# Fetching 54 of a graph kernel's gathered tiles row by row from SyncE and ScalarE

## The reference

```python
h = jnp.maximum(_layernorm(x, axis=-1), 0.0)
# layer 1: mean of h[src] over each node's edges, beside h itself, times W
# layer 2: theta = h[dst] - h[src]; w = sigmoid(relu(theta @ W1 + b1) @ W2 + b2)
#          segment_sum(w * theta, dst) + indeg * (h @ W4 + b4)
# layer 3: mean of relu(h @ Wp.T + bp)[src], linear, elu, normalised by row
# layer 4: all_h = einsum('ni,rio->rno', h, weight)
#          segment_sum(all_h[etypes, src] * norm, dst) + h @ loop_weight
```

## Time and profile before

| What | Value |
|---|---|
| Median of 3 runs | 5245.48 us (5244.3 to 5245.74) |
| The profiled execution: its own time | 5255.77 us |
| Its span | 5253.4 us |
| Busy: PE, DVE, ACT, POOL | 73%, 56%, 30%, 70% of the span |
| Layer 2's gathers | from 976.9 us |
| Layer 4's gathers | from 3685.7 us to 5241.6 us |

### The profile page before, as it was taken

The page is one execution under the profiler, slowest core; times in us unless marked ns, Lnnn a source line. Parts: engine busy times, 40 slices in busy tenths (PEclk is TensorE's granted clock), DMA queues, the critical chain, the costliest instruction groups (busy, mean ns, idle before and its releaser), DMA issues.

```text
span 5253.4 us, 75208 instructions
## 1 busy us (share of the span) xinstructions
PE 3851.4 (73%) x22393; PEld 2977.7 (57%) x22393; DVE 2942.4 (56%) x9882; ACT 1575.8 (30%) x5791; POOL 3668.8 (70%) x3899
## 2 busy tenths in 40 slices
PE   3889999665666556566665488879899999999544
PEld 3345555655565555555555455445677777777443
DVE  7998876665555566666666744444544433333232
ACT  5555443433333333333333401132112222221000
POOL 5345553677777777777777477757777777777776
PEclk7799999877777777877778799989999999998655
DMA  4234443555555555555555556556111111111222
GB/s 124 69 123 141 145 145 125 166 156 158 157 157 157 157 156 158 159 159 158 159 161 161 153 191 201 200 178 244 52 50 51 51 51 50 51 51 52 53 73 53
DMA packets 303264, 663.89 MB, mean 126 GB/s; under 512 B 70592, under 2 KB 152924, under 8 KB 293388
## 3 DMA queue, kind: packets, MB, share of 16 engines
q0 software_dynamic: 155152, 369.61, 25.7%
q1 hardware_dynamic: 145692, 288.54, 16.3%
q10 hardware_dynamic: 2016, 0.92, 0.1%
HBM read 545.40 MB, written 113.38 MB: 125 GB/s over the span
## 4 chain that ended last, share of the span: by engine, by line
POOL 48%; PE 21%; issue 17%; DVE 9%; DMA 2%; ACT 2%; DVEq 1%; SPq 0%; ACTq 0%; POOLq 0%
POOL rows L1535 40%; POOL third L1535 8%; PE ps L2721 6%; PE ps L2618 3%; PE ps L2706 3%; PE ps L2630 2%; PE ps L2679 2%; DVE tmp L2019 2%; PE ps L2567 1%; PE ps L2686 1%; DVE oneh L1928 1%; DVE turned_words L2020 1%; DVE rows L2020 1%; DMA rows<-tab_hp,idx_src 1%; ACT h L1710 1%
## 5 line engine op out<-in xcount | busy, mean ns | idle before, releaser
L1535 POOL DMA_INDIRECT rows<-tab_rel,third x1203 | 1190.4, 990 | 366.7 <-issue 364.0
L1535 POOL DMA_INDIRECT rows<-tab_hp,idx_src x1120 | 1083.5, 967 | 345.2 <-issue 335.9
L2744 PE MATMUL ps<-third 128*128 128x128 f32 x3126 | 626.4, 363 | 729.4 <-DVE third L2049 728.7
L1535 POOL DMA_INDIRECT rows<-tab_h,idx_src x790 | 772.2, 977 | 541.2 <-PE ps L2686 276.2
L2744 PEld LDWEIGHTS ps<-third 128*128 128x128 f32 x3126 | 548.3, 264 | 790.5 <-DVE third L2049 789.5
L1758 ACT ACTIVATE turned_words<-turned_words 128x128 f32<-128x128 f32 x1563 | 463.2, 297 | 1251.0 <-DVE turned_words L2062 1251.0
L2721 PE MATMUL ps<-third,h 128*128 128x385 bf16 (+1 forms) x3626 | 742.7, 335 | 44.3 <-DMA h<-cnt_d 24.6
L2679 PE MATMUL ps<-oneh,rows 128*128 128x128 f32 x2406 | 403.2, 320 | 262.8 <-DMA rows<-tab_rel,third 160.1
L2679 PEld LDWEIGHTS ps<-oneh,rows 128*128 128x128 f32 x2406 | 352.5, 225 | 330.3 <-issue 183.2
L1535 POOL DMA_INDIRECT third<-tab_hp,idx_src x443 | 426.9, 964 | 135.0 <-issue 133.8
L2721 PEld LDWEIGHTS ps<-third,h 128*128 128x128 bf16 x3626 | 351.5, 100 | 293.8 <-issue 29.6
(11 more groups left out here) (305 smaller groups left out, 5685.6 us busy)
## 6 DMA issues: line engine op xcount, KB each, us to landing
third<-dst_flat SPq DMA_DIRECT2D x390, 256.0 KB, 3.5
cnt_d<-h SPq DMA_DIRECT2D x37, 1568.0 KB, 5.8
h<-cnt_d SPq DMA_DIRECT2D x37, 1568.0 KB
tab_rel<-third SPq DMA_DIRECT2D x49, 512.0 KB, 3.1
rows<-tab_rel,third POOLq DMA_INDIRECT x1203, 2.5
rows<-tab_hp,idx_src POOLq DMA_INDIRECT x1120
rows<-tab_h,idx_src POOLq DMA_INDIRECT x790
third<-tab_hp,idx_src POOLq DMA_INDIRECT x443
```

Of the source, the lines that this page charges most:

```text
L1535: pool.indirect_dma_start(out=to[:, t, 0:n], out_offset=None, in_=table[:, :], in_offset=bass.IndirectOffsetOnAxis(ap=idx[:, col:col + 1], ...
L2744: last = pe.matmul(ps_t[sl][:, t * P:(t + 1) * P], onehT[:, sl, t * P:(t + 1) * P], pwin[:, st["v"] % 2, :], start=True, stop=True)
```

## The change

In 37 groups the last tile is no longer gathered by POOL, but fetched by SP: 19 in layer 2 (groups 20, 40, ... 380) and 18 in layer 4 (groups 108, 124, ... 380). In 17 more groups of layer 4 (116, 132, ... 372) ACT fetches it. In the 17 turns up to two turns before such a group, each turn has a step `single_rows`: load eight indices from one partition into eight registers, then eight DMAs of one row each, with the row's address from its register, into a staging tile (two for each engine and layer). At the group's own turn a step `single_copy` waits for all 128 rows and for the slot, and copies the tile into its slot with one DMA. The users of the group, DVE's `hidden` in layer 2 and PE's scatter, wait for that copy (`s_moved`) too. The indices come by small DMAs of SP: 19 before layer 2's first window, and 35 in the step `late` ahead of the loads that were there, each of 128 single words, one from each partition's row of `parked[0]`. In layer 4 the row work lies in each of the 16 turns between one single tile and the next, in layer 2 in 16 of 20.

```diff
+SINGLES = {1: (("sp", 20, 20),), 3: (("sp", 18, 16), ("act", 26, 16))}
+ROW_LOAD = 8
...
+            def single_rows(g):
+                for who in singles:
+                    for j, at in enumerate(singles[who]):
+                        r0 = (g - (at - P // ROW_LOAD - 1)) * ROW_LOAD
+                        if 0 <= r0 < P:
+                            if r0 == 0:
+                                single_full[who, j] = s_single[layer, who][j % 2].up(16 * P)
+                            free = n_moved[singles[who][j - 2]] if j > 1 and r0 == 0 else None
+                            plan.append(("single_rows", dict(layer=layer, who=who, j=j, r0=r0, free=free)))
...
             for turn in range(turns):
                 tails[:] = [tail for tail in tails if next(tail, "end") != "end"]
+                single_rows(g0 + turn)
...
                 elif kind == "late":
                     sp.wait_ge(s_pack.handle, st["pack"])
                     sp.wait_ge(s_park.handle, s_park.value)
+                    with nc.allow_non_contiguous_dma(reason="one index of each partition"):
+                        for k, g in enumerate(single_groups[3]):
+                            t = g * TPG + TPG - 1
+                            sp.dma_start(idx_single[3][k:k + 1, :].bitcast(U32), parked[0][:, t:t + 1].rearrange("p o -> o p")
+                                         ).then_inc(s_rowidx.handle, 16)
...
+                    for k, g in enumerate(single_groups[1]):
+                        t = g * TPG + TPG - 1
+                        sp.dma_start(idx_single[1][k:k + 1, :], ins["src"][t * P:(t + 1) * P].rearrange("(o e) -> o e", o=1)
+                                     ).then_inc(s_rowidx.handle, 16)
+                    sp.wait_ge(s_rowidx.handle, 16 * len(single_groups[1]))
...
-                    for t in range(tiles[g]):
+                    for t in range(st["n"]):
...
+                elif kind == "single_rows" and st["who"] == "act":
+                    layer, j, r0 = st["layer"], st["j"], st["r0"]
+                    table, full = tables[layer][0], s_single[layer, st["who"]][j % 2]
+                    to = single_at[layer, st["who"]][j % 2]
+                    if st["free"]:
+                        act.wait_ge(st["free"][0].handle, st["free"][1])
+                    at = row_at_single[layer, st["who"]] + j
+                    act.load(row_regs, idx_single[layer][at:at + 1, r0:r0 + ROW_LOAD])
+                    for r in range(ROW_LOAD):
+                        row = act.snap(row_regs[r], min_val=0, max_val=table.shape[0] - 1)
+                        act.dma_start(to[r0 + r:r0 + r + 1, :], table[bass.ds(row, 1), :]).then_inc(full.handle, 16)
+                elif kind == "single_copy" and st["who"] == "act":
+                    layer, j, sl = st["layer"], st["j"], st["slot"]
+                    act.wait_ge(s_single[layer, st["who"]][j % 2].handle, st["full"])
+                    if st["free"]:
+                        act.wait_ge(st["free"][0].handle, st["free"][1])
+                    act.dma_start((rows_hp if layer == 1 else rows_at)[sl][:, st["t"], 0:tables[layer][0].shape[1]],
+                                 single_at[layer, st["who"]][j % 2]).then_inc(s_moved[layer, st["who"]][j % 2].handle, 16)
...
                     pe.wait_ge(s_row[slot].handle, st["row"])
+                    if st["moved"]:
+                        pe.wait_ge(st["moved"][0].handle, st["moved"][1])
```

More of the change, by code:

```diff
@@ L372, in gnn_program @@
         s_off = sem("s_off")
+        s_rowidx = sem("s_rowidx")
+        s_moved = {(layer, who): [sem(f"s_moved{layer}{who}{k}") for k in range(2)] for layer in SINGLES for who, _, _ in SINGLES[layer]}
+        s_single = {(layer, who): [sem(f"s_single{layer}{who}{k}") for k in range(2)] for layer in SINGLES for who, _, _ in SINGLES[layer]}
         s_key3 = sem("s_key3")
@@ L851, in plan_edges @@
             n_bc, n_pw, n_oneT, n_expand, n_hid, n_z, n_gate = ({} for _ in range(7))
+            singles, single_of, single_full, n_moved = {}, {}, {}, {}
+            for who, first, step in SINGLES.get(layer, ()):
+                singles[who] = list(range(g0 + first, ng - ROW_LOAD, step))
+                single_of.update((g, (who, j)) for j, g in enumerate(singles[who]))
+            def single_rows(g):
[7 more added lines that the diff above has]
+                            plan.append(("single_rows", dict(layer=layer, who=who, j=j, r0=r0, free=free)))
             def gather(g):
@@ L856, in gather @@
                 sl = g % slots
-                n_row[g] = s_row[sl].up(16 * tiles[g])
-                plan.append(("gather", dict(layer=layer, g=g, slot=sl, free=slot_free.get(sl))))
+                n_row[g] = s_row[sl].up(16 * (tiles[g] - (g in single_of)))
+                plan.append(("gather", dict(layer=layer, g=g, slot=sl, free=slot_free.get(sl), n=tiles[g] - (g in single_of))))
+                if g in single_of:
+                    who, j = single_of[g]
+                    n_moved[g] = s_moved[layer, who][j % 2], s_moved[layer, who][j % 2].up(16)
+                    plan.append(("single_copy", dict(layer=layer, who=who, j=j, slot=sl, t=tiles[g] - 1, free=slot_free.get(sl),
+                                                     full=single_full[who, j])))
             def onehot(g):
@@ L878, in scatter @@
                 plan.append(("scatter", dict(layer=layer, g=g, v=v, slot=g % slots, sums=sums, one=n_one[g], row=n_row[g],
-                                             first=first, last=last, add=n_gadd.get(v - banks, added_before if layer == 3 else 0))))
+                                             first=first, last=last, add=n_gadd.get(v - banks, added_before if layer == 3 else 0),
+                                             moved=n_moved.get(g))))
                 if last:
@@ L1111, in hidden @@
                 n_hid[g] = s_hid.up()
-                plan.append(("hidden", dict(g=g, slot=g % slots, expand=n_expand[g], row=n_row[g], diff=s_diff.up(),
+                plan.append(("hidden", dict(g=g, slot=g % slots, expand=n_expand[g], row=n_row[g], moved=n_moved.get(g), diff=s_diff.up(),
                                             z=n_z.get(g - 2, 0))))
@@ L1365, in general_tensor @@
                     last.then_inc(q["scat"], 1)
+        single_groups, row_at_single = {}, {}
+        for layer in SINGLES:
+            single_groups[layer] = []
+            for who, first, step in SINGLES[layer]:
+                row_at_single[layer, who] = len(single_groups[layer])
+                single_groups[layer] += range((0, 0, 0, HEAD_END)[layer] + first, ng - ROW_LOAD, step)
+        n_rowidx = 16 * sum(len(groups) for groups in single_groups.values())
         def sync_program(sp):
+            row_regs = [sp.alloc_register(f"row{k}") for k in range(ROW_LOAD)]
             sp.wait_ge(s_pad.handle, n_pad)
@@ L1578, in scalar_program @@
             act.wait_ge(s_const.handle, n_const)
+            row_regs = [act.alloc_register(f"row{k}") for k in range(ROW_LOAD)]
             off_regs = [act.alloc_register(f"off{k}") for k in range(OFF_LOAD)]
@@ L1667, in scalar_program @@
                 elif kind == "edges_begin":
+                    if st["layer"] == 3:
+                        for k in range(3):
+                            if st["tab"][k]:
+                                act.wait_ge(s_tab[k].handle, st["tab"][k])
+                        act.wait_ge(s_rowidx.handle, n_rowidx)
                     act.wait_ge(s_mm.handle, st["mm"])
```

37 lines of the change are left out of this document (35 added, 2 removed).

## The result

The changed kernel takes 5284.81 us (median of four runs, 5282.99 to 5287.13) against 5245.61 us (5244.3 to 5247.63) before: 0.75% slower, ratio 1.0075, 95% interval 1.0057 to 1.0092. Two more comparisons gave 1.0060 (1.0044 to 1.0077) and 1.0081 (1.0064 to 1.0098). Forecast were 5213 us, with 0.62 on faster. The time is inside the range of 5175 to 5300, but on the other side of the kernel before.

A forecast was written before the change was run, and what follows sets the result against it. POOL's gathers were taken to bound layers 2 and 4, with PE close behind. Terms -24 - 45 + 35 + 2 = -32 us, taken from a median 10 us below the 5255.77 us execution, gave 5213 us; range 5175 to 5300.

The forecast's parts named there:

- POOL's pace: Layers 2 and 4: POOL sets the pace; 19 gathers fewer save 24 us, 35 fewer save 45 us.
- SyncE is hidden in layer 2: Layer 2: SP needs 81 us per 20 turns against POOL's 100.5 us, so its row work costs nothing.
- c: Issuer's time for one row fetched in layers 2 and 4: 0.47 us on SP, 0.49 us on ACT.
- The copy into the slot is one DMA per 20 turns, two turns before DVE needs it: SP's copy of the finished tile in layer 2, taken as hidden, without cost.
- the prediction's own formula: Layer 4's dense part: ACT's rows, copies and waits sum to 1092 us against 1017 us at POOL's pace.
- rival 1: Layer 4: all of ACT's added work hidden, no loss, 5178 us; chance 0.22.
- The 35 us of loss in the sum: Layer 4's dense part: ACT 75 us over POOL's pace, of which the slots' lead takes up 40 us.
- what slack is worth: Layer 4's dense part: eight groups of lead in the slots take up the first 40 us of lag.
- The index copies: 35 copies in `late`, 0.43 + 0.04 us each, 16.5 us mostly covered by SP's free time; 2 us, 0 to 5.
- Rival 2: Layer 4: ACT becomes the bound, slower than before from c = 0.51; 5309 us at 0.55, 5500 at 0.67; chance 0.22.
- Rival 3: Layers 2 and 4: one-row copies held back by their completions, c 0.81, over 6200 us; chance 0.04.
- Rival 4: `late`: index copies of single words slow, 35 x 2.38 = 83 us, +63 after cover, 5276 us; chance 0.03.

The follow-up runs named there:

- both_b: Changed kernel with ScalarE's slot copy a turn earlier and the 35 index copies behind SyncE's relation-table stores; three such runs on B: ratios 1.0733, 1.0714, 1.0736.

## Why the prediction was wrong

**What held.** POOL's pace: layer 2 gained 32 us for the 24 forecast. The 8 more are gathers that got shorter, 966 to 961 ns in the mean (x 1544 = 8 us); why they did isn't shown. SyncE is hidden in layer 2: DVE waited 11.8 us for its fetches. After the dense part PE came up again, and the last stretch is 35 us shorter. The cost of a row was too high, if anything. ScalarE's and SyncE's rows on A (ns min/median/max):

```profile
L1530 SPq TENSOR_LOAD <-key x592: 527/734/1357, 983.4 to 5222.7; - x198
...
L1533 SPq DMA_DIRECT2D key<-tab_rel x2304: 224/225/359, 3657.0 to 5226.6; - x192
```

```profile
L1806 ACTq TENSOR_LOAD <-key x272: 565/827/1363, 3732.0 to 5185.4; - x136
...
L1809 ACTq DMA_DIRECT2D key<-tab_rel x2176: 223/224/628, 3732.8 to 5189.5; - x198
```

225 ns where the sum had 251 + 28 and, for ACT, 20 more. Eight rows of SyncE take 3.19 us, so c is (3.19 - 0.23)/7 = 0.42 us for 0.47. ScalarE's run of 32 rows shows 4.22 us for eight rows and their load: less the load's 0.83 that is 0.42 a row for 0.49. The load of eight registers is 0.73 to 0.83 us for 0.55. The figure that I set against my 251 ns, 512 cycles for one DMA copy instruction (the Trainium skill, DMA: Bandwidth & Descriptors, "Why a DMA increments its semaphore by 16 and not by 1", an estimate of 0.43 us), does not hold here: 4736 one-row DMAs of SyncE and 2176 of ScalarE took half of it in the median (224 to 228 ns).

**The step that failed** is one sentence: "The copy into the slot is one DMA per 20 turns, two turns before DVE needs it", priced at nothing. That was for SyncE in layer 2, where it is right. ScalarE's copies in layer 4 got no sentence at all. Yet each stands in ScalarE's program behind the eight rows of its turn, PE's scatter waits for it, and POOL waits for the slot that this scatter frees. With the measured durations the prediction's own formula gives 200 x 4.22 + 190 = 1034 us for ScalarE, 17 over the 1017 of POOL's pace and well under the 40 that the slots take up: nothing lost, rival 1, 5178 us. As a sum of durations ScalarE's work does fit. What it is not is in time: by the order of the plan each copy stands behind 4.2 us of rows that begin when PE is already at the scatter, and PE has only 7% of slack. The runs showed 69 us of such waits in the dense part in place of nothing.

That the time lies inside the range is luck. The 35 us of loss in the sum stood for a ScalarE with too much work, which did not come; the real loss has another cause and happens to be of a size that the range covers.

**The other term that failed** is what slack is worth. The prediction let the slots take up 40 us of lag, once. The lag was used up (POOL's waits begin before 4200 us), and from then on each wait of PE was a wait of POOL, with the granted clock down from 1.00 to 0.96 on top. No term priced the clock: the slower matmuls are about 27 us of the 69 above.

**The index copies** were put at 2 us, 0 to 5, and cost 12 to 14 us. Thirty-five of them took 23.23 us, 0.66 each, not 0.47:

```profile
3477.78 23.23 SPq L1469 DMA_DIRECT2D key<-parked_rel  x35
...
3502.64 15.20 SPq L1482 DMA_DIRECT2D tab_pb<-h  x13
```

The cover was there, as forecast: before, SyncE waited 19.8 of the 25.6 us of the stores for ACT's h, now 2.4. But the stores, which now stand close behind the copies and each other, took SyncE twice as long each (before, then after, then with the copies moved away, in `both_b`):

```profile
L1436 SPq DMA_DIRECT2D tab_pb<-h x13: 372/403/2118, 3512.8 to 3537.9; - x13
```

```profile
L1482 SPq DMA_DIRECT2D tab_pb<-h x13: 776/857/3326, 3502.6 to 3517.0; - x13
```

```profile
L1484 SPq DMA_DIRECT2D tab_pb<-h x13: 372/403/1593, 4167.9 to 4193.0; - x13
```

So 15.2 us remain of the 25.6, not 6, and 23.2 less 10.4 is 12.8 us: what the landing of the table moved.

**The rivals.** Rival 2 came nearest: PE waits for ScalarE and the kernel is slower. But it was priced through c, from 0.51 on, and c is 0.42. Rival 3 did not come. Rival 4's mechanism did, at under a third of its price per copy.

**What stays open.** The sum over the dense part (copies 56, evictions 20, slower matmuls 27, less 34) is read from traces, and its parts repeat in two more. That the kernel would win with the late copies taken away is argued from it, not shown. The earlier copy stands ahead of two turns' rows, at least 8.4 us earlier by the 4.2 us of each, which is more than the waits of up to 6.9 us; on B it left none of them in the dense part, and on A it never ran. How much would then be left through ScalarE's row work, which stands ahead of its evictions (PE's waits for these are 20 us more on A, and layer 4 is 88 us longer by the rows on B), isn't known. Nor is it known what makes chips B slow. There, SyncE's queue gets stuck for up to 1.4 us at instructions that need nothing, 7,624 added waits cost 81 us, and the row fetches of layer 2, with as many instructions, 211 to 227. Whether the rest is their transfers or the kind of their instructions wasn't separated.

## What to carry to other kernels

When an engine with idle time takes over work, add up not only its busy time but also where in its order each result is handed on: who waits for that instruction, how long before need it is issued, and how much slack the waiting engine has in that stage. Placing the hand-over a turn earlier, ahead of the engine's other work, took these waits out of the dense part on B; what it gains was not measured. Near a second engine at 93%, removing work from the first is worth no more than the second's waits for it, here 25 us in 900, and a new wait is charged as idle time and once more through the clock. Waits of 34 us were free in a stage where PE was over half idle.

## What was unexpected of the hardware

- A DMA of one row of 512 or 1024 bytes from a register's address takes its queue 224 to 228 ns, less than the 251 ns of a fixed row of 256 bytes and than the 320 of SyncE's copies of line 1476 or the 452 of ScalarE's of line 1575. Copies that collect 128 single words, one from each partition, take 597 ns (568 to 1472).
- With ten short waits, most of 6 us, in a stretch where PE had been 93% busy, its mean granted clock went from 1.00 to 0.96, and its matmuls from 276 to 283 and from 498 to 505 ns. After one of them it was 0.68 for five us.
- In some comparisons the same program took 14% longer, and instructions were no longer free: 7,624 waits on a semaphore that already stood cost 81 us there, and 1.5 us, within the error, in the others. The changed kernel was 0.6 to 0.8% slower than before on the one kind, its nearest relatives 7% on the other. A change that trades one instruction of POOL for 400 of SyncE or ScalarE is exposed to that.
